# Layer-0 attention: scores and maxima as 64-row products, two heads on the two halves of the array

## The reference

```python
q = (hidden_states @ Wq.T).reshape(B, S, NUM_HEADS, HEAD_DIM).transpose(0, 2, 1, 3)
k = (hidden_states @ Wk.T).reshape(B, S, NUM_KV_HEADS, HEAD_DIM).transpose(0, 2, 1, 3)
v = (hidden_states @ Wv.T).reshape(B, S, NUM_KV_HEADS, HEAD_DIM).transpose(0, 2, 1, 3)
...
scores = jnp.einsum('bhqd,bhkd->bhqk', q, k) * scale
causal = jnp.triu(jnp.full((S, S), -jnp.inf, dtype=scores.dtype), k=1)
scores = scores + causal[None, None]
probs = jax.nn.softmax(scores, axis=-1)
out = jnp.einsum('bhqk,bhkd->bhqd', probs, v)
out = out.transpose(0, 2, 1, 3).reshape(B, S, NUM_HEADS * HEAD_DIM)
return out @ Wo.T
```

## Time and profile before

| | |
|---|---|
| median of 3 runs | 1519.43 us (1514.69 to 1521.86) |
| the profiled execution | 1523.38 us |
| its span in the profile | 1521.7 us |
| TensorE, products | 1279.1 us busy (84%) |
| TensorE, weight loads | 758.2 us (50%) |
| VectorE | 1002.2 us (66%) |
| ScalarE | 692.8 us (46%) |
| GpSimd | 378.7 us (25%) |
| layer 0's attention | 38.8 to 652 us of the span |

### The profile page before, as it was taken

The page is one execution under the profiler, slowest core; times in us unless marked ns, Lnnn a source line. Parts: engine busy times, 40 slices in busy tenths (PEclk is TensorE's granted clock), DMA queues, the critical chain, the costliest instruction groups (busy, mean ns, idle before and its releaser), DMA issues. The chain is left out here.

```text
span 1521.7 us, 20305 instructions
## 1 busy us (share of the span) xinstructions
PE 1279.1 (84%) x7132; PEld 758.2 (50%) x7132; DVE 1002.2 (66%) x1750; ACT 692.8 (46%) x1319; POOL 378.7 (25%) x243
## 2 busy tenths in 40 slices
PE   4688898989898989858999968337998888789998
PEld 3344444444454544346888855323443333257886
DVE  4466656555656553267999985747677666357998
ACT  2232524343343433344666664411566556425664
POOL 0035463645454646700000000302111111020000
PEclk9699999989999989968999988755899989868998
DMA  3101202020211010005766710032222220102220
GB/s 104 40 15 34 48 15 49 18 48 15 52 28 44 15 44 15 15 11 119 157 149 154 151 41 1 2 56 81 46 62 51 47 47 20 43 22 77 76 104 28
DMA packets 51471, 81.54 MB, mean 54 GB/s; under 512 B 16748, under 2 KB 34452, under 8 KB 47444
## 3 DMA queue, kind: packets, MB, share of 16 engines
q1 hardware_dynamic: 51004, 79.40, 21.6%
q10 hardware_dynamic: 384, 1.05, 0.6%
HBM read 63.75 MB, written 5.68 MB: 46 GB/s over the span
## 5 line engine op out<-in xcount | busy, mean ns | idle before, releaser
L1356 PE MATMUL ps<-qA 128*128 128x512 f32 x960 | 253.1, 400 | 15.4 <-POOL qA L1466 10.5
L631 DVE TENSOR_REDUCE mraw<-ps 128x1 f32<-128x512 f32 (+3 forms) x304 | 193.5, 659 | 96.9 <-PE ps L510 51.4
L735 ACT ACTIVATE shared<-ps 128x512 f32<-128x512 f32 (+1 forms) x216 | 119.9, 567 | 254.7 <-PE ps L543 247.4
L1071 DVE TENSOR_REDUCE mraw<-ps 128x2 f32<-128x1024 f32 (+3 forms) x160 | 173.8, 1114 | 71.7 <-PE ps L979 47.0
L1356 PEld LDWEIGHTS ps<-qA 128*128 128x128 f32 x960 | 181.9, 192 | 64.8 <-POOL qA L1466 12.2
L1126 ACT ACTIVATE shared<-ps 128x512 f32<-128x512 f32 (+2 forms) x320 | 154.4, 560 | 128.7 <-PE ps L995 128.4
L504 PE MATMUL ps<-kH,qA 128*128 128x512 f32 (+3 forms) x384 | 140.8, 420 | 51.3 <-DVE mraw L631 27.4
L542 PE MATMUL ps<-qA,kH 128*128 128x512 f32 (+3 forms) x384 | 166.3, 443 | 5.7 <-DMA qB<-mT 5.2
L765 POOL TENSOR_TENSOR VP<-VP,shared 128x2048 f32<-128x2048 f32 (+3 forms) x40 | 129.7, 3243 | 67.1 <-ACT shared L735 64.8
L1420 ACT CAST qA<-shared 128x512 fp32r<-128x512 f32 x160 | 99.3, 621 | 92.5 <-DVE shared L1558 91.0
L1368 PE MATMUL ps<-qA,kH 128*128 128x512 f32 x480 | 136.1, 392 | 4.1 <-DVE qA L1482 4.1
(11 more groups left out here) (250 smaller groups left out, 1928.6 us busy)
## 6 DMA issues: line engine op xcount, KB each, us to landing
shared<-comb SPq DMA_DIRECT2D x92, 256.0 KB, 4.4
qB<-qA SPq DMA_DIRECT2D x16, 512.0 KB, 4.8
rB<-a0rec_dram SPq DMA_DIRECT2D x60, 128.0 KB, 2.9
shared<-comb SPq DMA_DIRECT2D x7, 1024.0 KB, 4.5
rB<-a1rec_dram SPq DMA_DIRECT2D x28, 128.0 KB, 2.6
e0wUp<-in_w SPq DMA_DIRECT2D x48, 64.0 KB, 4.6
qA<-q_split SPq DMA_DIRECT2D x24, 128.0 KB
q_split<-qA SPq DMA_DIRECT2D x4, 512.0 KB
```

The lines of the kernel that those rows point to most:

```text
L631: nc.vector.tensor_reduce(out[:, h0:h0 + n_h, qt % 4], src, AX, ALU.max).then_inc(w_free, 1)
L735: nc.scalar.activation(probs(n)[:, hs[0]:hs[-1] + 1, lo:512], src, ACT.Exp, scale=scale)\
L1071: nc.vector.tensor_reduce(out[:, :, js[0]:js[-1] + 1, qt % 4], src, AX, ALU.max).then_inc(x_free, 1)
L1356: ins = nc.tensor.matmul(bank[0:M, :], w[par][:, at:at + M], h[:, cols], start=(r == 0), stop=(r == 2))
```

## The change

Query heads are held two side by side: heads 0 and 1 on the two halves of the partitions, heads 2 and 3 likewise behind them. `qH`, `qL` and the rows of maxima `mR` are views of `qA` and `qB` in that form, and a tile `oneRow` has a row of ones at partitions 0 and 64. `qB` is zeroed once.

- Scores: for two heads (`ps`, one pair, or both pairs where a unit has at most 256 columns) four factors, kH x qH, kH x qL, kL x qH and oneRow x mR, each a 64-row product on each half of the array, into two banks. Two slots of two banks take the place of three banks, and one exponential covers both banks.
- Maxima: only kH x qH, a 64-row product on each half, into the two work banks together; the mask comes as two parts on two halves; one reduction covers both banks. A `max` job counts as two banks in `w_free` and takes banks 0 and 1 both; other jobs take one.
- Projections: one high copy and one low subtraction of 128 partitions for two heads. The DMA copy to `qB` and the waits for it are gone.
- Sums: a job of its own (`sum`) in a work bank, the first fill of step 6 for qc 0 and of step 2 of the next group for qc 1; GpSimd's first addition of the next chunk waits for that job.
- Fills: the values are a part of the step too, so fills are cut over the score parts and a last share behind the values.
- The values' banks are 6 and 7.

```diff
@@ parts, plan
+        plan.setdefault(NU * g + 3 + LAG + 1, []).insert(0, ("sum", g, 0, 0))
+        plan.setdefault(NU * (g + 1) + LAG, []).insert(0, ("sum", g, 1, 0))
...
+        banks.append(banks[-1] + (2 if job[0] == "max" else 1))
...
-        heads = score_jobs(n) if n < STEPS else [()]
+        pairs = (score_jobs(n) if n < STEPS else []) + [None]
         fills = due.get(n, [])
-        size = -(-len(fills) // len(heads))
-        return [(hs, fills[size * i:size * (i + 1)]) for i, hs in enumerate(heads)]
+        cuts = [-(-len(fills) * i // len(pairs)) for i in range(len(pairs) + 1)]
+        return [(ps, fills[cuts[i]:cuts[i + 1]]) for i, ps in enumerate(pairs)]
@@ TensorE, a job
-                    bank = k.bank(idx % 2)
-                    if idx >= 2:
-                        pe.wait_ge(w_free, idx - 1)
+                    bank = work_bank(idx)
+                    taken = banks[idx] if kind == "max" else banks[idx] - 1
+                    if taken > 0:
+                        pe.wait_ge(w_free, taken)
...
-                        for i in range(n_h):
-                            ins = nc.tensor.matmul(bank[:, i * width:(i + 1) * width],
-                                                   k.qA[par][:, h0 + i, qt * P:(qt + 1) * P],
-                                                   k.kH[par][:, ch * 512:ch * 512 + width], start=(i == 0),
-                                                   stop=not diagonal, skip_group_check=True)
+                        for at in range(n_p):
+                            for i in range(2):
+                                ins = nc.tensor.matmul(work[:, i, at * width:(at + 1) * width],
+                                                       k.qH[par][half(i), ps.start + at, qt * P:(qt + 1) * P],
+                                                       k.kH[par][half(i), ch * 512:ch * 512 + width], start=(at == 0),
+                                                       stop=not diagonal, skip_group_check=True)
...
+                    elif kind == "sum":
+                        pe.wait_ge(added, additions[NU * g + (4 if qc == 0 else NU)])
+                        for h in range(REP):
+                            ins = nc.tensor.matmul(bank[CT * h:CT * (h + 1), :], k.ones[:, 0:CT], k.P64_sum[:, h, :],
+                                                   start=True, stop=True, skip_group_check=True)
+                        ins.then_inc(w_full, 1)
@@ TensorE, scores
-                        pe.wait_ge(qb_ld[qc], 16 * (g + 1))
-                    if s >= SCORE_BANKS:
-                        pe.wait_ge(p_done, s - SCORE_BANKS + 1)
+                    if s >= SCORE_SLOTS:
+                        pe.wait_ge(p_done, s - SCORE_SLOTS + 1)
...
-                    for at, h in enumerate(hs):
-                        out = score_bank(s)[:, at * w:(at + 1) * w]
-                        nc.tensor.matmul(out, k.kH[par][:, keys], k.qA[par][:, h, cols], start=True, stop=False)
-                        ins = nc.tensor.matmul(out, k.kL[par][0:hd + 1, keys], k.qB[par][0:hd + 1, h, cols],
-                                               start=False, stop=True)
+                    factors = ((k.kH[par][:, keys], k.qH[par]), (k.kH[par][:, keys], k.qL[par]),
+                               (k.kL[par][:, keys], k.qH[par]), (k.oneRow[:, :], k.mR[par]))
+                    for at, (left, right) in enumerate(factors):
+                        for i in range(2):
+                            out = score_banks(s)[:, i, 0:n_p * w].rearrange("p (a q) -> p a q", a=n_p)
+                            ins = nc.tensor.matmul(out, left[half(i), :], right[half(i), ps, cols], start=(at == 0),
+                                                   stop=(at == 3))
@@ TensorE, the steps
-                    if n >= LAG:
-                        values(n - LAG)
-                        if closes(n - LAG):
-                            sums(n - LAG)
+                        elif n >= LAG:
+                            values(n - LAG)
+                        for idx in fills:
+                            job(idx)
@@ VectorE
-                        for i in range(2):
-                                h = 2 * (j - 1) + i
-                                ins = nc.vector.tensor_tensor(k.qA[par][hd:2 * hd, h, cols],
-                                                              bank[i * hd:(i + 1) * hd, :],
-                                                              k.qA[par][0:hd, h, cols].bitcast(F32), ALU.subtract)
+                        nc.vector.tensor_tensor(low, bank, high.bitcast(F32), ALU.subtract).then_inc(w_free, 1)
...
-                        nc.vector.tensor_reduce(out[:, h0:h0 + n_h, qt % 4], src, AX, ALU.max).then_inc(w_free, 1)
+                        nc.vector.tensor_reduce(out[:, :, ps, qt % 4], src, AX, ALU.max).then_inc(w_free, 2)
...
+                    elif kind == "sum":
+                        dve.wait_ge(w_full, idx + 1)
+                        if g or qc:
+                            dve.wait_ge(sum_ld[1 - qc], 16 * REP * (g + qc))
+                        nc.vector.tensor_copy(k.S64[:, :], bank).then_inc(w_free, 1)
@@ ScalarE
-                            src = score_bank(s)[:, 0:len(hs) * (512 - lo)].rearrange("p (a q) -> p a q", a=len(hs))
-                            nc.scalar.activation(probs(n)[:, hs[0]:hs[-1] + 1, lo:512], src, ACT.Exp, scale=scale)\
-                                .then_inc(p_done, 1)
+                            src = score_banks(s)[:, :, 0:n_p * (512 - lo)].rearrange("p i (a q) -> p i a q", a=n_p)
+                            dst = probs(n).rearrange("p (a i) q -> p i a q", i=2)[:, :, ps, lo:512]
+                            nc.scalar.activation(dst, src, ACT.Exp, scale=scale).then_inc(p_done, 1)
@@ GpSimd
-                        pool.wait_ge(summed, 2 * g + qc)
+                        before = index["sum", g, 0, 0] if qc else index["sum", g - 1, 1, 0]
+                        pool.wait_ge(w_full, before + 1)
@@ SyncE
-                    sp.dma_start(k.qB[g % 2][0:hd, :, cols].bitcast(F32), k.qA[g % 2][0:hd, :, cols].bitcast(F32))\
-                        .then_inc(qb_ld[qc], 16)
...
-                    sp.wait_ge(o_dve, 2 * g + qc + 1)
+                    sp.wait_ge(sums_out, 2 * g + qc + 1)
```

More of the change, by code:

```diff
@@ L359, in stage_attention64 @@
     LAG = 2
-    SCORE_BANKS = 3
+    SCORE_SLOTS = 2
     U = 1 + REP // 2
@@ L378, in score_jobs @@
     def score_jobs(n):
-        size = max(1, 512 // (512 - unit_lo(n)) // 2 * 2) if 512 - unit_lo(n) <= 256 else 1
-        return [tuple(range(h, h + size)) for h in range(0, REP, size)]
+        return [slice(0, 2)] if 512 - unit_lo(n) <= 256 else [slice(0, 1), slice(1, 2)]
     first_score = [0]
@@ L395, in max_jobs_of @@
             for ch in range(qc + 1):
-                n = 512 // keys_in(qt, ch)
-                out += [(qt, ch, h, n) for h in range(0, REP, n)]
+                out += [(qt, ch, slice(0, 2))] if keys_in(qt, ch) <= 256 else \
+                    [(qt, ch, slice(p, p + 1)) for p in range(2)]
         return out
@@ new lines, in job @@
+                        if diagonal:
+                            for part in range(2):
+                                for i in range(2):
+                                    ends = work[:, i, 0:n_p * width].rearrange("p (a w) -> p a w", w=width)
+                                    ins = nc.tensor.matmul(ends[:, :, width - P:width], k.halves[half(i), 0, part, :],
+                                                           k.halves[half(i), 1, part:part + 1, :]
+                                                           .broadcast_to((64, n_p, P)), start=False,
+                                                           stop=(part == 1), skip_group_check=True)
@@ L568, in values @@
                     ins.then_inc(pv_done, 1)
-                def sums(n):
-                    pe.wait_ge(added, additions[n + 1])
-                    for h in range(REP):
-                        ins = nc.tensor.matmul(SUMS[CT * h:CT * (h + 1), :], k.ones[:, 0:CT], k.P64_sum[:, h, :],
-                                               start=True, stop=True, skip_group_check=True)
-                    ins.then_inc(summed, 1)
                 for idx in due[-1]:
@@ L704, in high @@
                     cols = slice(qc * 512, (qc + 1) * 512)
-                    if j == 0:
-                        ins = nc.scalar.copy(k.kH[par][:, cols], bank)
-                    else:
-                        for i in range(2):
-                            ins = nc.scalar.copy(k.qA[par][0:hd, 2 * (j - 1) + i, cols], bank[i * hd:(i + 1) * hd, :])
-                    ins.then_inc(q_hi, 1)
+                    high_part = k.kH[par][:, cols] if j == 0 else k.qH[par][:, j - 1, cols]
+                    nc.scalar.copy(high_part, work_bank(idx)).then_inc(q_hi, 1)
                 def copy_out(n):
```

112 lines of the change are left out of this document (59 added, 53 removed).

## The result

| | before | after |
|---|---|---|
| median | 1518.66 us (4 runs, 1514.69 to 1521.86) | 1560.80 us (4 runs, 1555.79 to 1565.93) |
| ratio | | 1.0279 (95%: 1.0236 to 1.0322) |
| the profiled execution, its span | 1523.38, 1521.7 us | 1562.32, 1560.6 us |

The kernel is slower by 42 us; the forecast was 20 slower, 1540. First the stretches that answer to the earlier trace rows: group 0 in two parts, two steady groups, the last group.

The account below looks back on a forecast made before the run. TensorE was taken as the bound, by its products and gaps. Steady-group terms summed to 74.5 us, a walk gave 73.9: +7 over six groups; with group 0 +11 and the last +2, +20: median 1540, range 1500 to 1580.

Parts of the forecast that it names:

- Maxima on TensorE: Steady group: half the serial columns for maxima, 9,216 fewer, as two 64-row products run at one time: -4.3 us.
- The division: Steady group, step 9: L667 may wait for GpSimd's addition: +1.6 us, bounds 0 and 3.
- The switches: Steady group: 17 added switches between 64-row and other products at 0.19 each: +3.2 us, bounds 0 and 0.34 each.
- Removed waits: Steady group: waits at projections, the 2.91 with the half clock behind it, and short gates go: -11.7 us, bounds -6.5 and -12.
- rounds with the division: Steady group: serial rounds of maxima that take both work banks, +14.6 us, and the division behind GpSimd's addition, +1.6.
- short gates: Steady group before the change: short TensorE waits at nearly every maximum, about 5 us, replaced by the rounds.
- The fold: Steady group, step 6: L602 keeps its collision with GpSimd's addition, but its later transpose removes the 2.91 us wait.
- Group 0: First group: rounds in the open +1.3, 14 rounds in four steps +5, group 1's jobs +4.7; together +11 us.
- rival C: Steady groups, steps 6 to 10: idle rounds drop TensorE's clock under 0.9, +7 x 6 on the forecast, 1582 us; chance 0.15.
- Rival A: Faster: loads and drains hide as one half loads while the other multiplies, 6 us a group, 1500 us; chance 0.18.
- B: No change: the division misses the addition (-1.6 x 6) and group 0's rounds cost nothing (-11), 1520 us; chance 0.17.
- D: Pairs run one after the other, score columns double, about +20 us a group, some 1660 us; chance 0.05.

Follow-up runs that it names:

- the last run: The changed kernel with one score slot, two pairs of work banks, one job a part, and value products in two halves behind the score parts: 1461.77 us, 0.9621 of before.

## Why the prediction was right, and where it was mis-sized

The sign, the mechanism and the place were right: rounds made serial by the two-bank job, in steps 6 to 11 and in group 0. The round (1.78 for 1.8), the wait behind a score part (0.46 for 0.6) and the blocked division (some 1.5 for 1.6) measured near their price. The sums made of them were less exact, and partly right by luck, as the next points say.

- Maxima on TensorE, -4.3 a group: busy time, in which products that run together count once, fell from 17.0 to 9.7 us in the two steady groups whose steps are shown; the direction holds, and as busy time the gain is larger than priced.
- The division: L682 ends after the addition where they meet (311.12 and 2.38, against 307.88 and 4.54) and takes 1.22 us where they don't. The Trainium skill (SBUF — State Buffer, Who interferes with whom) has an exclusive lock on a port pair that GpSimd shares with VectorE instructions of two SBUF inputs; this row agrees. That would let the whole addition be waited for; the division came when 3.2 of its 4.54 us had passed.
- The switches, +3.2 a group: no run shows this term by itself; the two runs with few maxima show only that it and the small gains come to nothing together. The Trainium skill (TensorEngine Tiling (Array Packing), Key Properties) says that a change of tiling mode drains TensorE; no run here shows the size of that.
- Two banks a maximum: the Trainium skill (TensorEngine Tiling (Array Packing), Gotcha 1: PSUM Pressure) says that different row tiles write to different PSUM banks, which is why one job for both halves takes two. No run here puts both halves into one bank; what it cost to hold both work banks is shown by the run with one score slot, at 75 us.
- Removed waits, -11.7, and rounds with the division, +16.2: as far as idle time shows them, both were priced too high, and the errors go against each other. That the sum came out near is in this part luck. TensorE's waits for reductions at its maxima, before and after, in the same two groups (total us, times, longest):

```profile
PE ps L504 <- DVE mraw L631: 4.2, 4, 2.9
...
PE ps L519 <- DVE mraw L641: 10.3, 10, 2.9
```

  Before, TensorE is idle for 6.9 us of that group in all; the two large waits named (2.91 and 1.92) are 4.8 of it. So the "short gates" of about 5 us, which were what the estimate by paces left over, can be 2.1 us of idle time at most; the rest, if it was there, lay within busy time, which no row separates. After, 10.3 us before maxima and 1.4 more before a projection make 11.7.
- The fold: it was to keep its collision with GpSimd's addition. In each of the six steady groups it took 0.17 to 0.18 us instead of 2.78, because it came some 0.05 us ahead of the addition:

```profile
289.54 0.18 DVE L619 COPY mmax<-mraw 128x16 f32<-128x16 f32 x1
289.59 4.53 POOL L780 TENSOR_TENSOR VP<-VP,shared 128x2048 f32<-128x2048 f32 x1
```

  In group 0 it collided (139.30, 3.67 us). That the 2.91 is gone in steady groups is thus not shown to come from the later transpose. The waits on low parts fell from 19.2 us (L504 before, at L621) to 7.1.
- Steady groups, forecast +1.2 each, measured +2.8; with dummies +2.6. The last stretch (1.3 above its forecast) has most of what is missing.
- The last group, "+2": 42.1 us for 42.2 to its last step, and 1.1 us longer to the end of the attention.
- Group 0, the step that failed in size: "Together +11", measured +27.7 with its later start. With dummies it is 104.6 us, +10.9, at a mean clock of 0.93 (0.92 before), so the price of its rounds was right at the old clock, and the fall of the clock to 0.73 was left out of it. The traces had shown that place at 0.63 and 0.80, and I put the clock into rival C, for steps 6 to 10 of steady groups, where two of the six groups ran at 0.93 and took some 2 us more before the change too (73.9 us each). Small beside it, but priced at nothing: TensorE's waits for the rows of maxima, all in group 0, grew from 5.2 to 7.9 us (by the DMA into `qB`). The timeline of group 0 after the change:

```profile
150.10 3.64 PE L591 MATMUL ps<-shared 128*32 128x512 f32 x16
...
153.68 0.80 PE L519 MATMUL ps<-kH,qA 64*128 64x512 f32 x2
154.58 1.23 DVE L641 TENSOR_REDUCE mraw<-ps 128x2 f32<-128x1024 f32 x1 [4.09 <-PE ps L519]
155.86 0.79 PE L519 MATMUL ps<-kH,qA 64*128 64x512 f32 x2 [1.39 <-DVE mraw L641]
...
173.19 1.92 PE L591 MATMUL ps<-rB,shared 128*32 128x512 f32 x16
```

The same sixteen value products take 3.64 us at 150.10 and 1.92 at 173.19, the first behind waits for the reductions one after another, at a granted clock of 0.50, the second at 1.00. A round takes 2.18 us at the half clock (153.68 to 155.86) instead of 1.78: the reduction starts 0.90 behind the product and not 0.50, while the wait is 1.39 in both. So the low clock makes each round longer by 0.40. That the waits hold the clock down fits the run with dummies, but isn't the whole of it: with one bank a maximum TensorE is idle for 16.5 us of group 0 instead of 32.1, and the clock stays at 0.75.

Rival A fell: a first pair still takes 0.34. B fell: the division met the addition, and group 0 was no free place. C was right in that the clock cost more than was priced, but in group 0; its sign, a steady group under 0.9, didn't come (the lowest is 0.93). D fell with the pairs' pace.

## What to carry to other kernels

When a product is made faster by using two banks at once, count the banks before the columns: if the job then holds every buffer of its reader, what the products save comes back as waits. Where PSUM is full, try the second buffer on the chain whose reader is slower and has less between its turns (here the reduction, 1.23 us, rather than the exponential, 1.02), and spread the jobs so that each has other work behind it. Price waits in a stage that already runs at a low clock separately: in group 0 they cost more than their length.

## What was not expected of the hardware

Waits of 1.4 us, one behind another, left TensorE at 0.65 to 0.77 of its clock through all of group 0, while steady groups with waits of that length, mixed with long runs of products, kept 0.93 to 0.98. A wait of 2.5 to 2.6 us in each steady group of the last run was followed by a fall of the clock in four of them and by none in two. Products whose result nobody reads, put into those waits, made the kernel 17 us faster (1560.8 to 1543.4). Why the clock stays up in one and not in the other isn't settled by these runs.
